# Bias rows on 128 partitions, straight-line middle images and new instruction orders in a six-layer image kernel on one Trainium2 core

## What is computed

```python
x = x + deformable_conv3x3(_gn(x))        # 9 taps gathered at learned offsets, 4 cells each, + bias
x = x + sorted_self_correlation(_gn(x))   # 1024x1024 correlation per image, each row sorted, 128 ranks kept
t = _to_tokens(x)                         # 1024 tokens x 128
t = t + window_attention(_ln_t(t))        # windows 4, 16, 32, + bo
t = t + moe(_ln_t(t))                     # 8 experts, top 2, gelu
t = t + ssm(_ln_t(t))                     # conv of length 4 with bias, scan over the tokens
t = t + moe(_ln_t(t))                     # 8 experts, top 2, hidden size 341
```

## Time and profile before

| | |
|---|---|
| median of 3 runs | 4934.46 us (4929.53 to 4936.54) |
| the profiled execution's own time | 4926.88 us |
| its span from first to last instruction | 4925.1 us |
| mean granted TensorE clock | 0.893 of 2.4 GHz |
| instructions in the trace | 59870 |

### The profile page before, as it was taken

One profiled execution on the slowest core, in us unless ns is written; L12 is line 12 of the kernel. 1 busy time (PEld: TensorE's weight loads), 2 busy tenths in 40 slices (PEclk: granted clock), 3 DMA queues, 4 the chain that ended last, 5 costly groups with the idle time before them and its releaser, 6 DMA issues.

```text
span 4925.1 us, 59870 instructions
## 1 busy us (share of the span) xinstructions
PE 3975.1 (81%) x19410; PEld 2674.8 (54%) x19410; DVE 4278.7 (87%) x5380; ACT 2954.3 (60%) x7241; POOL 894.7 (18%) x580
## 2 busy tenths in 40 slices
PE   5747748989798988989798988989798987767587
PEld 3616424667456654567456654566456653545354
DVE  1098999999999999999999999999999999999521
ACT  4526526687467846687467846687467855555452
POOL 2317000242005300242005300242005210000000
PEclk8878869999899988999799988999799988978798
DMA  4314100232013210232013210232013210010001
GB/s 131 98 35 124 35 0 18 75 101 69 5 43 110 79 36 18 75 102 68 7 43 110 79 36 18 67 104 67 13 43 109 71 40 13 22 29 27 10 22 39
DMA packets 226079, 269.71 MB, mean 55 GB/s; under 512 B 26831, under 2 KB 188506, under 8 KB 225626
## 3 DMA queue, kind: packets, MB, share of 16 engines
q0 software_dynamic: 46080, 151.03, 10.6%
q1 hardware_dynamic: 179674, 114.65, 7.9%
...
## 4 chain that ended last, share of the span: by engine, by line
PE 38%; DVE 33%; issue 12%; ACT 9%; DMA 4%; POOL 3%; SPq 1%; DVEq 0%; another core or an unknown queue 0%; ACTq 0%; POOLq 0%
PE bank L597 6%; PE bank L1633 4%; PE bank L1628 4%; PE bank L1613 3%; PE bank L1298 3%; POOL gath L759 3%; DMA gath<-quads,idx 3%; DVE srt_b L873 2%; DVE srt_b L881 2%; DVE srt_a L796 2%; DVE srt_b L796 2%; PE bank L569 2%; PE bank L1225 2%; PE bank L1218 2%; DVE srt_a L893 2%
## 5 line engine op out<-in xcount | busy, mean ns | idle before, releaser
L759 POOL DMA_INDIRECT gath<-quads,idx x576 | 894.5, 1553 | 3083.4 <-DVE idx L722 2005.3
L597 PE MATMUL bank<-diag,gath 128*128 128x128 f32 x4608 | 612.4, 295 | 167.6 <-DMA gath<-quads,idx 166.8
L639 ACT ACTIVATE diag<-ident,w 128x128 f32<-128x128 f32 x2304 | 704.6, 393 | 20.3 <-DVE w L737 20.2
L597 PEld LDWEIGHTS bank<-diag,gath 128*128 128x128 f32 x4608 | 591.3, 210 | 203.1 <-DMA gath<-quads,idx 126.9
L1613 PEld LDWEIGHTS bank<-e2w,act 128*128 128x128 f32 (+1 forms) x3072 | 409.8, 198 | 161.7 <-issue 157.3
L1628 PE MATMUL bank<-mu_t,e2w 128*128 128x512 f32 (+1 forms) x768 | 424.0, 635 | 86.4 <-DMA e2w<-moe_w_t 39.9
L1633 PE MATMUL bank<-gated_u,e2w 128*128 128x512 f32 (+1 forms) x768 | 426.1, 638 | 34.2 <-DVE act L1713 31.9
L1713 DVE TENSOR_TENSOR act<-act,bank 128x512 f32<-128x512 f32 (+1 forms) x384 | 261.3, 680 | 180.0 <-PE bank L1633 159.5
L1613 PE MATMUL bank<-e2w,act 128*128 128x128 f32 (+1 forms) x3072 | 415.0, 282 | 1.6 <-DVE act L1713 1.6
L873 DVE TENSOR_TENSOR srt_b<-srt_a 128x1024 f32<-128x1024 f32 x192 | 351.3, 1830 | 1.2
L881 DVE TENSOR_TENSOR srt_b<-srt_a 128x1024 f32<-128x1024 f32 x192 | 351.0, 1828 | 0.0
...
## 6 DMA issues: line engine op xcount, KB each, us to landing
...
e2w<-moe_w_t SPq DMA_DIRECT2D x128, 42.5 KB
...
```

The lines of the kernel that those rows point to most:

```text
L597: ins = T.matmul(FB[q % 2][:, k * P:(k + 1) * P], gath[:, g % 2, k, s * C:(s + 1) * C], diag[:, g % 2, 4 * k + s], start=(s == 0), stop=(s ...
L639: ins = SC.activation(diag[:, g % 2, n], ident[:], ACT.Copy, scale=w[:, n:n + 1])
L759: pool.indirect_dma_start(gath[:, g % 2, k], None, quads, bass.IndirectOffsetOnAxis(idx[:, TG * g + k:TG * g + k + 1], 0)).then_inc(sem["g ...
```

## The change

The three bias tiles become 128 partitions high, with the bias copied to each of them (three loads with a broadcast), and the matmuls take the unit matrix as weights. In the setup, the product of the value bias with the output weights, which is added to bo, is made on 128 partitions as well: one VectorE product more, and a matmul with 128 columns of weights for one with a single column. The two hardware loops become Python loops, so that bodies 2 to 6 are written out, still with the order strings of "full". All strings of the early, full, late and drain bodies change but SP_early and SP_drain; the fill's stay. No step is added or taken away: each string has the same count of each letter as before. Of the strings, those that the text speaks of are shown:

```diff
     ACT_early=(
...
-        "FFFFFFFFFFFFFFCFFFFCCFFCFFCCCFFFFFCCFFFCCFCCFCCFFCCFFFFFFFFFFFFCCCCCCCCCCCCCCCCCCCCCCCCCCCCCCCCC"
+        "FFFFFFFFFFFFFFFCFFFCCFFCFFCCCFFFFFFCCFFCCFCCFCCFCFCFFFFFFFFFCFCFFCCCCCCCCCCCCCCCCCCCCCCCCCCCCCCC"
...
     DVE_early=(
         "SSSSSSSSSSSSSSSSSSSSSSSSSSSSSSFFSSFSSFSSSSSSSSSSSSSSSFSSSFSSFFSSFSSSSSSSSSSSSSSSSSSSSSSSSSSSSSSS"
-        "SSSSSSSSSSSSSSSSSSSSSSSSSSSCSSCSSSSSSSSSSCCSSCCSSSSSFSSCFSSCFSSFSSSFCSSCSSCSSCSSCSSSCSSSSSSSSSSS"
-        "SSSSCSSCSSSSSSSSSSSCCSSCSSCSSCSSCCSSCSSCSSCSSSSSCSSSSCCSSSSCCSSSSCCSSSSCSSCSSCSSSSSSSS"
+        "SSSSSSSSSSSSSSSSSSSSSSSSSSSSSCSSSSSSCSSSSSSCCSSSSSCCSSSSFSSCFSSSCFSSFSSCFCSSCSSCSSSCSSCSSSSSSSSS"
+        "SSSSSSSSCSSCSSSSSSSSSSSCSSCSSCSSCSSCSSCCSSSCSSCSSCSSSSCSSSSCCSSSSCCSSSSCCSSSSCSSCSSSCS"
     ),
     SP_full=(
-        "CCCMMMCCCCCCCCMMFFMMMMMMMMCMCCCMCMMMF"
+        "CCCMMCMCFCCFCCCCMMMMMMMMMCCMCCCMFMMMM"
     ),
...
     DVE_full=(
-        "MCMSSCSSMSSSSMSSCCMSSCCMSSMSSMSSSCSSCMSSMSSCMCSSSCMCSSCMCSSMSSSSSSSMSSSSSSSSCMFFCMSSFSSSFSSSSCSS"
-        "CMSSCMSSCMCSSCCSSSCMSSCMCSSSSCMSSCCSSMFSSCCMFSSFFSSSCCMFSSCSSMCSSMSSCMSSSSMSSMSSMMSSMSSSSMSSMSSM"
-        "SMSMSMSCSSCSSMSSSSMSSCCMSSCMSSCMSSSSSMSSCSSCSSSSSMSSCMCSSCMCSSCSSCMSSSMSSSSMSSSSMSSMSSSSSMSSSSSS"
-        "CMSSCMSSMSSSSSSSCSSCMSSCMSSCMCSSCCMSSCMSSSCMCSSSSCSSCCSSSSCCFFSSCCFSSSSCFSSCFSSCSSSSSSSSSS"
+        "MCSSCMSSSSSSSSCCMSSCCMSSMSSMSSSCMSSCMSSSSCSSSCMSSCMFCFCMSSCFMSSFMSSSSSMSSSSSSMSSSSMSSSSSMSSCSSCM"
+        "SSMSSSSSSSSSCSSCMSSCSSCFMCFSSCCFFMSSCFMSSCSSSCMSSMSSCSSCMSSCSSCCSSMSSCMCSSCMSSCSSSSCMSSMSSMMSSMS"
+        "SSSCSSCMSSSSMSSMSSMSSCCMSSCMCSSSSSSSCMSSCMSSSMSSCSSCMSSCMSSCSSSCMSSCSSMSSSSMSSMSSSSSSSSSSSSSCMSS"
+        "SSSCMSSSSMSSSSSSCCSSCMSSMSSSCFMCFCCFSSCMSSCFMCSSFMSSCSSCMSSCMSSSSCCMSSSSCCMSSCMSSCMSSCSSSS"
     ),
...
     DVE_late=(
-        "MCSSCMSSSSSSSSSSCCMSSCCMSSMSSSMSSCMSSCMSSSSSCSSCMCSSCMCSSCMSSSSSMSSSSMSSSSMSSSSSSSMSSCMSSCMSSSSM"
-        "SSSSSCSSCSSCMSSCMCSSCCMSSCMSSCMCSSSSSCMSSMSSCCMSSSSCCMSSMSSCCMSSCMSSCMSSCMMSSMSSSSMSSMSMSMSMSMCS"
-        "SCSSMSSSSMSSCCMSSCCMSSMSSCSSSCMSSSSCMCSSCMCSSSCMCSSSSMSSSSMSSSSSMSSSSSSCMSSCMSSSMSSSSSSCSSCMSSCM"
-        "SSCMCSSSCCSSCMSSCMCMSSCSSMSSCCMSSMSSCSSSCSSCCSSSSCSSCSSCSSSSSSSSSSSSSSSSSSSS"
+        "MCSSCMSSSSSSSSCCMSSCCMSSMSSMSSSCMSSCMSSSSCSSSCMSSCMSSCMSSCSSCMSSSMSSSSMSSSSSSSSSSSCMSSCMSSMSSSSS"
+        "SSSSCSSCMSSCMSSCMSSCSSCCMSSCMSSCMSSSCSSSSMCSSMSSCCMSSSSCSSCMSSSSCCMSSSSCMSSCSSCMSMSSMMSSSCMSSCSS"
+        "SSSSMSSCCMSSCCMSSMSSSMSSCMSSCSSSSSMSSCMSSCMSSCMSSCMSSSCMSSCSSMSSSSMSSMSSSSSSSSSSSMCSSCMSSSSSMSSS"
+        "SSSCCSSCMSSCMSSCMSSCCSSSCMSSCMSSCMSSSSCMSSSSCCMSSCMSSCSSCMSSCMSSSSCMSSCSCSSS"
     ),
...
@@ -167,17 +167,17 @@
         om_w = sb("om_w", [P, TAPS, OM])
         om_b = sb("om_b", [OM, 1])
         conv_w = sb("conv_w", [P, TAPS, C])
-        conv_bias = sb("conv_bias", [1, C])
+        conv_bias = sb("conv_bias", [P, C])
         wqkvo = sb("wqkvo", [P, 4, C])
         bqk = sb("bqk", [P, 3])
-        bo_row = sb("bo_row", [1, C])
+        bo_row = sb("bo_row", [P, C])
         router1 = sb("router1", [P, E8])
         router2 = sb("router2", [P, E8])
         b1 = sb("b1", [P, E8])
         b2 = sb("b2", [E8, C])
         w_zdt = sb("w_zdt", [P, ZDT])
         w_xbc = sb("w_xbc", [P, CONVK, XBC])
-        cb_row = sb("cb_row", [1, XBC])
+        cb_row = sb("cb_row", [P, XBC])
         dt_bias = sb("dt_bias", [P, HEADS])
         neg_a = sb("neg_a", [P, HEADS])
         dskip = sb("dskip", [P, HEADS])
@@ -387,12 +387,12 @@
             load(om_w[:], A["L0_conv_om_kernel"].rearrange("a b c o -> c (a b) o"))
             load(om_b[:], A["L0_conv_om_bias"].rearrange("(o a) -> o a", a=1))
             load(conv_w[:], A["L0_conv_kernel"].rearrange("(t c) f -> c t f", c=C))
-            load(conv_bias[:], A["L0_conv_bias"].rearrange("a b c f -> (a b c) f"))
+            load(conv_bias[:], A["L0_conv_bias"].rearrange("a b c f -> (a b c f)").partition_broadcast(P))
             for n, w in enumerate("qkvo"):
                 load(wqkvo[:, n], A["L2_attn_W" + w])
             for n, w in enumerate("qkv"):
                 load(bqk[:, n:n + 1], A["L2_attn_b" + w].rearrange("(c a) -> c a", a=1))
-            load(bo_row[:], A["L2_attn_bo"].rearrange("(a c) -> a c", a=1))
+            load(bo_row[:], A["L2_attn_bo"].partition_broadcast(P))
             load(router1[:], A["router1_t"])
             load(router2[:], A["router2_t"])
             load(b1[:], A["b1_t"])
@@ -400,7 +400,7 @@
             load(w_zdt[:], A["w_zdt_t"])
             for k in range(CONVK):
                 load(w_xbc[:, k], A["w_xbc_t"])
-            load(cb_row[:], A["L3_attn_conv_b"].rearrange("(a c) -> a c", a=1))
+            load(cb_row[:], A["L3_attn_conv_b"].partition_broadcast(P))
             load(dt_bias[:], A["L3_attn_dt_bias"].partition_broadcast(P))
             load(neg_a[:], A["L3_attn_A_log"].partition_broadcast(P))
             load(dskip[:], A["L3_attn_Dp"].partition_broadcast(P))
@@ -438,10 +438,11 @@
             V.tensor_scalar(bqk[:, 0:1], bqk[:, 0:1], -SCALE, None, ALU.mult)
             V.tensor_copy(ident_h[:], ident[:])
             V.tensor_scalar(minus[:], ident[:], -1.0, None, ALU.mult)
+            V.tensor_scalar(tc[:, 1], ones[:], bqk[:, 2:3], None, ALU.mult)
             V.tensor_copy(future_h[:], tc[:, 0]).then_inc(prep, 1)
             yield
             dve.wait_ge(prep, 4)
-            V.tensor_tensor(bo_row[:], bo_row[:], CB[0][0:1, 0:C], ALU.add)
+            V.tensor_tensor(bo_row[:], bo_row[:], CB[0][:, 0:C], ALU.add)
             V.tensor_scalar(neg_a[:], neg_a[:], -1.0, None, ALU.mult).then_inc(prep, 1)
             dve.wait_ge(prep, 5)
             yield
@@ -458,7 +459,7 @@
         def pe_prep(pe):
             pe.wait_ge(loaded, 16 * n_loads[0])
             pe.wait_ge(prep, 3)
-            T.matmul(CB[0][0:1, 0:C], bqk[:, 2:3], wqkvo[:, 3], start=True, stop=True).then_inc(prep, 1)
+            T.matmul(CB[0][:, 0:C], tc[:, 1], wqkvo[:, 3], start=True, stop=True).then_inc(prep, 1)
             yield
             pe.wait_ge(prep, 5)
             yield
@@ -602,7 +603,7 @@
                     pe.wait_ge(sem["cols"], img("cols", i, g + 1))
                     out = FB[1][:, 0:C]
                     T.matmul(out, ident[:], x_tok[:, t], start=True, stop=False)
-                    T.matmul(out, ones[0:1, :], conv_bias[:], start=False, stop=False)
+                    T.matmul(out, ident[:], conv_bias[:], start=False, stop=False)
                     for k in range(TAPS):
                         ins = T.matmul(out, cols[:, k], conv_w[:, k], start=False, stop=(k == TAPS - 1))
                     ins.then_inc(sem["conv"], 1)
@@ -949,7 +950,7 @@
         uall = u_t[:, 3:3 + HALF]
 
         def row4(row):
-            return row.unsqueeze(1).to_broadcast([1, UT, C])
+            return row.unsqueeze(1).to_broadcast([P, UT, C])
 
         def stats(dve, link, src, st, m, name):
 
@@ -1050,7 +1051,7 @@
                 yield
             T.matmul(CB[0][:], ident[:], flat(tc[:]), start=True, stop=False)
             T.matmul(CB[0][:], ident[:], flat(u), start=False, stop=False)
-            T.matmul(CB[0][:], ones[0:1, :], row4(bo_row[:]), start=False, stop=False)
+            T.matmul(CB[0][:], ident[:], row4(bo_row[:]), start=False, stop=False)
             yield
             pe.wait_ge(sem["ctx_sb"], unit("ctx_sb", i, h))
             for t in range(UT):
@@ -1293,7 +1294,7 @@
                 if n >= 3:
                     pe.wait_ge(sem["zx_sb"], unit("zx_sb", i, h, n - 2))
                 if conv:
-                    T.matmul(out[:, 0:XBC], ones[0:1, :], cb_row[:], start=True, stop=False)
+                    T.matmul(out[:, 0:XBC], ident[:], cb_row[:], start=True, stop=False)
                     for k in range(CONVK):
                         ins = T.matmul(out[:, 0:XBC], u_t[:, t * P + k:t * P + k + P], w_xbc[:, k], start=False, stop=(k == CONVK - 1))
                 else:
@@ -1737,7 +1738,7 @@
             body(-1, True, False, False)
             body(0, True, True, False)
             body(1, True, True, True)
-            with eng.Fori(2, IMGS - 1) as i:
+            for i in range(2, IMGS - 1):
                 body(i, True, True, True)
             body(IMGS - 1, False, True, True)
             body(IMGS, False, False, True)
@@ -1778,7 +1779,7 @@
             body(-1, True, False, False)
             body(0, True, True, False)
             body(1, True, True, True)
-            with sp.Fori(2, IMGS - 2) as i:
+            for i in range(2, IMGS - 2):
                 body(i, True, True, True)
             body(IMGS - 2, True, True, True, False)
             body(IMGS - 1, False, True, True)
```

More of the change, by code:

```diff
@@ L83 @@
+        "MFCCCCCCCCMCMCMFMMMFMMMMCMMMCMMMMCMMMFCMCMMFFCCMMMFMCCMMMFCMMMFCFCMMMFMFMMMFMMMMMFFFMMFCFCCFCFFF"
+        "CCCMCCCMMFMFMMFMMCCMMMFMFMMMFMMMFMMCMCMMCCMMFCMCCCMCCCMCCFCCCCCCCCCMCCMMCMFFMMMFCMMCCCCCCCCMCMCM"
+        "MMFMMMFMMMFFCMMMMFCMMMMMCMFMMMCCMFFMMMCCMMMFCCMMMFMFFCMMMCMMCMMMFFFFF"
     ),
```

(32 more changed lines are left out.)

18 lines of the change are left out of this document (6 added, 12 removed).

## The result

The kernel after takes 4944.17 us, the median of 12 runs (4930.7 to 4963.56), against 4933.61 for the kernel before in 12 runs on the same chip: a ratio of 1.0032 [1.0021, 1.0043]. It is 0.3% slower, and the forecast of 4884 (4848 to 4922) was wrong. The profiled execution took 4936.17 us, with a span of 4934.4 and a mean clock of 0.895.

The account below looks back on a forecast made before the run. VectorE was taken as the bound wherever an image is sorted. Terms 9.8 + 10.5 + 2.9 + 16 + 1.8 - 0.7 + 10 + 7 - 7 = 50.3 us off the median 4934.5 gave 4884, range 4848 to 4922.

Parts of the forecast that it names:

- the charge for new waits: VectorE's other waits (L1713, L1539, L1152) in bodies 1 to 7: 7 us slower in all, ends -25 and +50.
- Rival 3: SyncE's queue: cell writes delay weights of experts five to seven, TensorE stands in L1206; 12 over gives 4956; chance 0.14 with its like.
- the last of its signs: Sign that the forecast is wrong: SyncE's cell writes precede an idle TensorE at L1206.
- The wait at L1476: VectorE's wait for the projection, 35.4 us: bias rows take 16 us off, the full order's added S letters 10.
- The 10 us credited for it: Full order's extra sort letters before L1476: half of the remaining 19.4 us credited, ends 0 and 19.
- The bias rows: Full-height matmuls at L605, L1296, L1053: 2.9 us in the head, 16 at L1476, 1.8 in the tail, less 0.7 setup.
- The price of one place: One one-row matmul between two full ones costs TensorE 0.36 us extra, at 144 places.
- The tail: Last 324.8 us: one half's four rows and its bo row on the chain, 5 x 0.36 = 1.8 us gained.
- The setup's 0.7: Setup's three bias loads, small VectorE product and 128-column matmul: 0.7 us slower, ends 0 and 2.
- The straight-line code: Middle images without loops: 9.8 us for taken branches plus 10.5 us for register work gained.
- branch holes: VectorE's first instruction behind each taken branch waits 2.45 us; 9.8 us gained for four passes.
- The early order: VectorE's 13.2 us wait between the first LayerNorm's statistics and reciprocal: 7 us gained, ends 0 and 13.

## Why the prediction was wrong

**The step that failed** is the charge for new waits: "Relief in one place shows up elsewhere, so I charge 1 us for each of seven bodies: 7 us". They cost 76 us in the six full bodies (3355.1 against 3278.8 with the old strings): L1714 82.6 against 26.0 and L1540 27.3 against 6.0 make 78, less what other waits gave back. Rival 3 had the mechanism, the queue and the line, and the last of its signs came true: cell writes ahead of an idle TensorE at L1206. Its 12 us a body was an example; VectorE's pair of waits is 10.2 to 11.5. That its 4956 lies near the measured 4944 is luck, since it set a loss of 72 against a gain of 50, and the runs show 86 against 70. I gave it 0.14 on two arguments. "The letters leave some 20 us between F and the need": but TensorE was ready for the first load 10.6 us after its set of writes had begun, and for the next 11.0 us after the second set had; the sets hold the queue 10.3 and 10.8 us and a load takes 4 more. And "the same F letters come after 30 S in the early order without a wait" shows only that the normalised rows are there in time, not which loads stand behind the writes. That could have been read before: SyncE's string laid against TensorE's by number shows which load follows F, and when its matmul comes up.

**The wait at L1476** went wholly, as foreseen, but not by the letter count alone: with the new orders and one-row matmuls the first halves' products come after 10.9 us in every body, at the full clock, where they took 12.6 to 14.2. In the second halves, at an equal clock, the new orders alone took all 9.5 us of it away, so there the letters did cover. It was worth little, because VectorE reached the next wait earlier. The 10 us credited for it can at best be seen in the undisturbed bodies of the kernel with moved writes, 544.2 and 545.3 us against a mean of 3278.8 / 6 = 546.5 with all old strings.

**The bias rows**: right in mechanism and place, the size off. The sum had 20 us (2.9 + 16 + 1.8 - 0.7); they are worth 42. L1476 gave 22.9 in the six bodies of the kernel with all bias rows (30.6 to 7.7) where I had 1.1 x 12 = 13. The price of one place was right (0.36 foreseen, though its three terms add to 0.35; 0.39 found at L1296). What was missing is the clock: the first halves run their projection in part at half speed before and less so with full-height rows. The tail looks 6.9 us shorter (324.8 to 317.9), not 1.8, but here too the clock differs:

```profile
4599.80:4921.10 321.30, 257.58 (x1126) 163.41 (x1126) 78.56 (x214) 162.03 (x346) 0.00 (x0) 0.89 0.09 27
4564.50:4882.40 317.90, 253.63 (x1126) 161.58 (x1126) 78.58 (x214) 162.02 (x346) 0.00 (x0) 0.89 0.09 27
```

This is the tail with one-row matmuls (the kernel with the convolution's rows alone, which has none in its tail) and with full-height ones (all bias rows) at a clock of 0.89: 3.4 us apart. At 0.87 they are 1.9 apart (324.8 in the earlier trace rows, 322.9 in the kernel after). So some 2 to 3 us are the rows', near the 1.8, and the rest is the clock of that execution. The rest of the 42 lies in the bodies' other waits (32 us shorter in all, of which L1476 is 23) and the head, and isn't placed. The setup's 0.7 can't be seen. One reading was not exact: a full-height load of weights takes 190 ns at L1052, so the one-row load's 182 is a little less, not "no less".

**The straight-line code**: 20.3 foreseen, 24 measured on the kernel before; branch holes and the register work's 2.4 us of VectorE's busy time a body are gone. Beneath the new orders it gave nothing, which the forecast didn't consider.

**The early order**: 7 us foreseen, and right. In the kernel with the new early strings and old full ones, the wait of the earlier trace rows is

```profile
485.00 0.18 DVE L1074 RECIPROCAL lnsd<-lnsd 128x4 f32<-128x4 f32 x1 [6.14 <-ACT lnsd L1064]
```

It stands at 12.97 us in the kernel after, which runs the same instructions up to there. That is the exception: of the eight profiles with the new early strings six have 5.9 to 8.3 us and two 13.0 and 13.5, while the six with the old ones have 13.2 to 21.5.

**The sum as it came out**: -42 for the bias rows and -24 for the loops, together -70, and 86 for the orders: 16 us slower. The full strings alone lose 95 us (0.9839 to 1.0032), and the cell writes' place is nearly all of it: moved, it gives 86 back, though the gathers still cost some 12 us in four of six bodies of that profile. That cost is paid in some bodies and not in others, which would account for the spread of the runs (54 us between the fastest and slowest of the kernel with moved writes, 10 and 20 in the two with the old full strings).

**Left open**: what sets whether a body's gathers fall into the sort's stride; why the clock is back sooner in the first halves beside full-height SSM rows and beneath the new orders; whether the old SyncE string alone would heal the new orders. That wasn't tried: with it, I expect that expert loads and matmuls would wait for each other.
